# Cached attention: where the second unit of each row of four keeps its scores, and what TensorE waits for before it

## The reference

```python
q = rope(rmsnorm((x @ Wq.T).reshape(B, S, 32, 128)))        # 32 query heads
k = rope(rmsnorm((x @ Wk.T).reshape(B, S, 8, 128)))         # 8 key heads
v = (x @ Wv.T).reshape(B, S, 8, 128)
k_all = concat([k_cache[block_table], k], axis=1)           # 512 cached keys and 32 own ones
v_all = concat([v_cache[block_table], v], axis=1)
valid = (arange(512) < cache_seqlens) or own key
scores = einsum('bqhd,bkhd->bhqk', q, repeat(k_all, 4)) * SCALE
probs = softmax(where(valid, scores, -1e30))
o = einsum('bhqk,bkhd->bqhd', probs, repeat(v_all, 4))
x = x + second_attention(o @ Wo.T)                          # and then the mixing and feed-forward part
```

## Time and profile before

| what | value |
|---|---|
| median of 3 runs | 3037.3 us (3034.73 to 3038.21) |
| profiled execution, its own time | 3041.85 us |
| its span, first to last instruction | 3040.3 us |
| granted TensorE clock, mean | 0.998 of full speed |
| TensorE busy | 3002.2 us, 99% of the span |
| cached attention, first scores to last values | 600.1 to 1652.4 us |

### The profile page before, as it was taken

The page is one execution under the profiler, slowest core; times in us unless marked ns, Lnnn a source line. Parts: engine busy times, 40 slices in busy tenths (PEclk is TensorE's granted clock), DMA queues, the critical chain, the costliest instruction groups (busy, mean ns, idle before and its releaser), DMA issues.

```text
span 3040.3 us, 89884 instructions
## 1 busy us (share of the span) xinstructions
PE 3002.2 (99%) x36256; PEld 2329.9 (77%) x36256; DVE 1804.1 (59%) x3587; ACT 1552.2 (51%) x2949; POOL 605.7 (20%) x1462
## 2 busy tenths in 40 slices
PE   8999999899999999999999999999999999999999
PEld 7777778767776777776777888888888888888887
DVE  5777779477777777777775444432333333544544
ACT  6666655387777777777775222212333334322221
POOL 0000001355455455455451000000000000300000
PEclk9999999999999999999999999999999999999999
DMA  5333335577777776776776434312333333843311
GB/s 162 110 105 111 109 113 152 171 217 215 215 214 212 215 213 210 215 215 210 216 216 213 124 110 124 117 78 107 98 94 104 117 104 89 242 149 111 110 42 56
DMA packets 506645, 456.28 MB, mean 150 GB/s; under 512 B 33985, under 2 KB 470593, under 8 KB 501698
## 3 DMA queue, kind: packets, MB, share of 16 engines
q1 hardware_dynamic: 470402, 354.41, 39.0%
q0 software_dynamic: 35904, 96.85, 9.9%
HBM read 321.03 MB, written 130.02 MB: 148 GB/s over the span
## 4 chain that ended last, share of the span: by engine, by line
PE 77%; DVE 2%; issue 1%; ACT 0%; DMA 0%; DVEq 0%
PE ps_o L1007 17%; PE ps_scores L991 15%; PE s_ps L58 8%; PE s_ps L60 8%; PE s_ps L59 8%; PE s_ps_proj L58 5%; PE s_ps_proj L59 5%; PE s_ps_proj L60 5%; DVE masked L941 2%; PE s_ps_o L1531 1%; PE s_ps_scores L1507 1%; PE yv_ps L60 1%; PE yv_ps L59 1%; PE yv_ps L58 1%; PE s_ps L1706 0%
## 5 line engine op out<-in xcount | busy, mean ns | idle before, releaser
L1007 PEld LDWEIGHTS ps_o<-weights_t,v_all 32*128 32x128 f32 x17408 | 500.9, 187 | 59.2 <-issue 33.1
L991 PE MATMUL ps_scores<-k_slot,q_slot 128*32 128x288 f32 (+1 forms) x8192 | 526.4, 396 | 16.0 <-PEq L98 4.8
L1007 PE MATMUL ps_o<-weights_t,v_all 32*128 32x128 f32 x17408 | 526.5, 274 | 5.7 <-issue 4.1
L941 DVE CUSTOM_DVE_ANT_0 masked<-ps_scores,reach,scale_now 128x544 f32<-128x544 f32 x512 | 390.6, 763 | 237.4 <-PE ps_scores L991 234.4
L897 ACT ACTIVATE probs<-masked,shift 128x544 f32<-128x544 f32 x512 | 381.5, 745 | 109.2 <-DVE shift L941 94.3
L991 PEld LDWEIGHTS ps_scores<-k_slot,q_slot 128*32 128x32 f32 x8192 | 235.6, 109 | 261.6 <-DVE shift L941 98.5
L954 DVE STREAM_TRANSPOSE weights_t<-probs 128x544 f32<-128x544 f32 x512 | 376.5, 739 | 15.0 <-ACT probs L902 2.5
L902 ACT ACTIVATE probs<-probs,inv 128x544 f32<-128x544 f32 x512 | 376.3, 735 | 0.0
L1090 ACT ACTIVATE s_h_hi<-s_h_raw 128x2048 fp32r<-128x2048 f32 x64 | 122.7, 1919 | 486.7 <-PE s_ps L60 474.6
L84 POOL COPY k_slot<-k_pool 128x256 f32 x1024 | 354.7, 406 | 21.6 <-issue 21.0
L58 PE MATMUL s_ps_proj<-y_hi,s_w_hi 128*128 128x512 f32 x640 | 253.1, 395 | 0.0
(11 more groups left out here) (202 smaller groups left out, 4667.3 us busy)
## 6 DMA issues: line engine op xcount, KB each, us to landing
v_all<-vpool_in SPq DMA_DIRECT2D x1024, 128.0 KB, 2.9
qT_scratch<-k_pool SPq DMA_DIRECT2D x32, 1024.0 KB, 5.1
q_slot<-qT_scratch POOLq DMA_DIRECT2D x64, 512.0 KB, 3.7
oT_scratch<-o_t POOLq DMA_DIRECT2D x128, 256.0 KB, 5.0
s_h_raw<-oT_scratch SPq DMA_DIRECT2D x32, 1024.0 KB, 5.8
aT_scratch<-s_o_t SPq DMA_DIRECT2D x32, 1024.0 KB, 5.6
s_h_raw<-aT_scratch SPq DMA_DIRECT2D x32, 1024.0 KB
w_raw<-w_in SPq DMA_DIRECT2D x11, 1024.0 KB, 7.7
```

Of the source, the lines that this page charges most:

```text
L941: dve.tensor_tensor_reduce(masked[:, k % 2, :], ps_scores[:, k % 2, LOW:LOW + KEYS], reach[:, k // HK, :], scale_now[:, k // HK, k % HK:k ...
L991: m = pe.matmul(ps_scores[q * S:(q + 1) * S, k % 2, cols], q_slots[j][:, head, r * S:(r + 1) * S], k_slots[j][:, pages, head * PSIZE:(head ...
L1007: m = pe.matmul(ps_o[:, q, 0:GS], v_all[rows, j, t, e * D:(e + 1) * D], weights_t[rows, g, :, t * S:(t + 1) * S], start=t == 0, stop=t == NPP)
```

## The change

The second unit of each row (r = 1) puts its scores in the first two banks of `ps_o`. The other three units share the two places of `ps_scores`: in an even row r = 0 and r = 3 take place 0 and r = 2 takes place 1, in an odd row the other way round. Unit r = 1 waits for the copy of the values that TensorE has just finished, in place of a `lowest`. Unit r = 2 waits for the `lowest` of r = 3 of the row before, and r = 3 for that of r = 0 of its own row. The values of a row get one more wait, for the `lowest` of the unit r = 1 whose scores stand in their banks. The order of the instructions on all engines and the transfers stay.

```diff
+        ps_lent = ps_o[:, 0:2, :].rearrange("p s n -> p (s n)")
+
+        def scores_place(n):
+
+            grp, r = n // G, n % G
+            return ps_lent if r == 1 else ps_scores[:, (grp + (r == 2)) % 2, :]
+
...
                 dve.wait_ge(scores_done, n + 1)
-                dve.tensor_tensor_reduce(masked[:, k % 2, :], ps_scores[:, k % 2, LOW:LOW + KEYS], reach[:, k // HK, :],
+                dve.tensor_tensor_reduce(masked[:, k % 2, :], scores_place(n)[:, LOW:LOW + KEYS], reach[:, k // HK, :],
...
-                if n >= 2:
-                    pe.wait_ge(shift_done, n - 1)
+                if n % G == 1:
+                    if n >= 3 * G:
+                        pe.wait_ge(o_copied, n // G - 1)
+                elif n >= G:
+                    pe.wait_ge(shift_done, n - 1 if n % G == 0 else n - 2)
+                elif n == 3:
+                    pe.wait_ge(shift_done, 1)
...
-                        m = pe.matmul(ps_scores[q * S:(q + 1) * S, k % 2, cols], q_slots[j][:, head, r * S:(r + 1) * S],
+                        m = pe.matmul(scores_place(n)[q * S:(q + 1) * S, cols], q_slots[j][:, head, r * S:(r + 1) * S],
...
                 pe.wait_ge(turned_w, grp * G + G)
                 pe.wait_ge(o_copied, grp + 1)
+                pe.wait_ge(shift_done, min((grp + 2) * G + 2, B * HK))
```

## The result

| kernel | median | lowest to highest | profiled execution | its span |
|---|---|---|---|---|
| before | 3037.3 us (4 runs) | 3034.73 to 3038.21 | 3041.85 us | 3040.3 us |
| changed | 3006.9 us (4 runs) | 3005.34 to 3016.11 | 3007.51 us | 3006.0 us |

The ratio is 0.9904, with a 95% interval of 0.989 to 0.9918: 30.4 us less by the medians, 34.3 us less from profile to profile. The forecast was 3005 us in a range of 2999 to 3014.

The account below looks back on a forecast made before the run. TensorE was taken to bound the stage, with two small holes a row. Removing them saves 31.9 us over 125 rows, plus 0.5 at the start: 32.4 off 3037.3 makes 3004.9 us, range 2999 to 3014.

Parts of the forecast that it names:

- What bounds the kernel, and the two holes of a row: TensorE bounds the stage; its score weights wait for `lowest` twice a row, 93.4 us in about 125 rows.
- The size of the holes: Scores to values take 3.81 us without holes; rows lose 0.20 (e = 1) or 0.31 us (e = 0), 31.9 us in all.
- The wait of r = 3: Fourth unit's wait for `lowest` of r = 0 of its own row: cover 0.8 us, costs nothing.
- The wait of r = 1 for the copy: Second unit's new wait: weights 0.08 to 0.13 us late, 0.06 to 0.11 to spare, costed at 0.
- The tolerance of 0.19: Fourth unit's weights went out 0.19 us late in the kernel before and its matmuls lost nothing; taken as a lower bound.
- The further wait of the values: Values' added wait for `lowest` of r = 1: cover 0.8 us, costs nothing if TensorE's queue holds the fourth unit's 32 instructions.
- The other engines: VectorE, ScalarE, SyncE and GpSimd keep idle time in the shorter rows; ScalarE keeps 0.62 us before the copy.
- The start of the stage: First three rows: a third place for scores lets the first values start up to 1 us earlier; 0.5 us taken.
- A: Copy's signal comes too late for r = 1: gives back 0.03 to 0.15 us a row, 3009 to 3024 us; chance 0.12.
- B: ScalarE becomes the bound as a late copy holds up r = 1; kernel slower, about 3055 us; chance 0.02.
- C: No gain: VectorE's chain through a row or the pages' transfers take over at the old pace, 3037 us; chance 0.03.
- D: Issue holes before the values' weights (28.5 us) shrink by up to a third, 10 us more gain, 2995 us; chance 0.04.

## Why the prediction was right, point by point

- **What bounds the kernel, and the two holes of a row.** Right, and shown by experiment: with the old wait of r = 2 the time is 3037.8 us again. Strictly the row had one hole in its matmuls, that of r = 2. Behind the other wait only the weights of r = 3 were late, and their matmuls kept step, as the prediction's own working says further down.
- **The size of the holes.** 3.81 us was worked out for a row without them, 3.80 is in the chain. 31.9 us were expected from the 125 rows, and between the first values and those of the 126th row 32.5 were found, of which 32.6 are regular. The rare holes, which are in every profile, cancel in this pair by luck (8.0 and 8.1 us); in the three later profiles of the changed kernel they are 4.7 to 6.4 us. The issue holes in front of the values' matmuls, 1.8 us before and 3.6 after, are between nothing and 1.6 us in the later profiles, so they are scatter and not a part of the change.
- **The wait of r = 3.** Right that it costs nothing. The cover of 0.8 us was counted to the matmuls; the weights of r = 3 go out at S + 2.56, and counted to them it is 0.5 to 0.6 us. But it isn't a side matter: left as it was, it would have eaten 23 of the 31 us.
- **The wait of r = 1 for the copy.** Right at a cost of 0. The lower bound of the signal, 0.06, was the true one (0.05). The upper one, 0.11 from the earlier trace rows, came from a wait with an instruction of its own in front, as the experiment with two waits showed. The tolerance of 0.19, taken from a wait for VectorE, was sound as far as it was tried: 0.12 late (S + 0.85) cost nothing in the row, 0.25 late (S + 0.98) cost 0.06. Between the two nothing was tried at this wait.
- **The further wait of the values.** Right, nothing, shown by itself. (The prediction added the 0.08 us of the read behind `lowest` to its 0.78; the two overlap, and it ends at S + 2.90, not S + 2.97.) That the fourth unit's instructions are handed on before it agrees with the 64 entries that the Trainium skill gives TensorE's queue (TensorE: Matmul & The Clock Gate, Architectural detail): no hole beyond the changeover stands in front of the values. The queue's depth was not measured.
- **The other engines.** Right: the idle time before the copy is 0.63 and 0.72 (0.62 was the forecast for the tighter row), SyncE still waits for TensorE (220.6 us in 56 places, 700 to 1580 us) and GpSimd for the copy (278.9 us in 63).
- **The start of the stage.** 0.5 us was taken, in bounds of 0 and 1; from the first scores to the first values it was 0.45 us (17.07 against 16.62). This pair can't confirm so small a number: the same stretch is 16.6 to 17.0 us in the three later profiles of the changed kernel and 17.9 in that of the kernel before with the further wait.
- **The rivals.** A is not in the changed kernel; it begins with a copy between 0.07 and 0.20 us later, by the two that were tried. B and C didn't happen. D, a gain from fewer issue holes, didn't either: those in front of the values' weights are 28.5 us before and 29.8 after. The median of the first four runs lies 2 us above the forecast, the three later ones within 1 us of it. That they agree so closely is in part luck, since the saving itself came out at 30.4, 30.9, 36.7 and 33.1 us against the forecast of 32.4.

## What to carry to other kernels

When one engine works 99% of a stage, look for holes in its starts, not its busy time: a hole of 0.2 or 0.3 us in an 8 us row was 1% of the program, and the unbroken spacing of its passes told its size to 2%. A buffer that is idle between its copy and its next use can serve as a third place for a short-lived tile; check the one new wait that this makes against the time at which the weights would go out, and how late they may be. If two waits in a row hold the same engine back, moving one of them only shifts the hole to the other.

## What the runs showed of the hardware that was not expected

- A wait carried by a weight load itself let it go 0.05 us after ScalarE's instruction ended. With a second wait in front of it, as a sequencer instruction of its own, it was 0.11 us, and the matmuls started another 0.03 later.
- A weight load may be 0.12 to 0.19 us late without moving its matmuls, in passes of 0.22 to 0.24 us. At 0.25 late they move, and the unit is 0.02 longer for cold weights.
- Cutting a copy of 512 columns (0.60 us) in two makes pieces of 0.38 us, the second of which starts 0.10 before the first ends, so that both together take only 0.66 us.
- Most kernels' runs differ by 6 to 11 us here, while the rows of their profiles have the same length. Between the slowest and the fastest of the four profiles of the changed kernel (3006.0 and 3000.6 us in span) 3.4 us lie in the rare holes of the 125 distances and 1.6 us in the last two rows of values. The holes over 0.42 us in the changed kernel's profiles end 1.25 to 1.49 us after a transfer of 16 KB on the queue for instructions.
- With under half of the transfer load the changed kernel's runs lay within 2.5 us and all but the last of its row distances were free of holes. A lower load isn't needed for close runs, though, nor does it ensure them: the kernel whose second unit waits twice had runs within 1.4 us with all pages, and the kernel before with fewer pages had runs 6.8 us apart and one hole of about 4 us.
